# Splitting the MLP, the query and the turned rows between the GELUs of a two-layer transformer kernel

## The reference

```python
h = shift_token(x)                       # channels 128..255 from the row before
q, k, v = split(h @ wqkv)                # 8 heads of 64
q, k = l2norm(q) * qs, l2norm(k) * ksc
q, k = rotary_xpos(q, k)                 # x * cos + rotate_half(x) * sin, scaled
o = local_attention(q, k, v)             # windows of 128, each looks at itself and the one before
x = x + o @ wo
h = layernorm(shift_token(x)) * lg + lb
a, g = split(h @ w1 + b1)                # hidden width 682, padded to 6 blocks of 128
x = x + (a * gelu(g)) @ w2 + b2
```

## Time and profile before

| | us |
|---|---|
| median of 3 runs | 4432.98 (4428.99 to 4451.38) |
| the profiled execution | 4428.6 |
| its span, first to last instruction | 4426.8 |
| busy PE | 3827.8 (86%) |
| busy DVE | 2947.5 (67%) |
| busy ACT | 2631.8 (59%) |
| busy POOL | 1870.1 (42%) |

### The profile page before, as it was taken

One profiled execution on the slowest core, in us unless ns is written; L12 is line 12 of the kernel. 1 busy time (PEld: TensorE's weight loads), 2 busy tenths in 40 slices (PEclk: granted clock), 3 DMA queues, 4 the chain that ended last, 5 costly groups with the idle time before them and its releaser, 6 DMA issues. The chain is left out here.

```text
span 4426.8 us, 87646 instructions
## 1 busy us (share of the span) xinstructions
PE 3827.8 (86%) x33070; PEld 2945.5 (67%) x33070; DVE 2947.5 (67%) x7093; ACT 2631.8 (59%) x5752; POOL 1870.1 (42%) x1453
## 2 busy tenths in 40 slices
PE   4899999999987489989989998958999898989987
PEld 2454554554543378777878877847878787878776
DVE  5677777777773566766676666636676767676774
ACT  1455555555555366666666666636666666666674
POOL 2123233232230344445454545424555555555554
PEclk6899999999997699999999999978999999999999
DMA  5334434434420200000000000020000000000000
GB/s 133 81 65 117 96 72 116 102 76 108 118 45 24 79 14 16 18 14 19 14 19 14 19 16 16 10 70 8 23 22 24 21 24 21 25 21 23 22 23 20
DMA packets 145440, 195.90 MB, mean 44 GB/s; under 512 B 21532, under 2 KB 119544, under 8 KB 145024
## 3 DMA queue, kind: packets, MB, share of 16 engines
q1 hardware_dynamic: 145024, 190.31, 16.8%
HBM read 113.66 MB, written 67.16 MB: 41 GB/s over the span
## 5 line engine op out<-in xcount | busy, mean ns | idle before, releaser
L728 ACT ACTIVATE a_e_t<-a_ring 128x1024 f32<-128x1024 f32 (+3 forms) x768 | 611.3, 809 | 524.2 <-PE a_ring L869 365.9
L1622 POOL TENSOR_TENSOR b_e<-b_e,b_share 128x512 f32<-128x512 f32 (+1 forms) x512 | 502.5, 989 | 965.4 <-DVE b_share L2060 965.3
L1050 DVE TENSOR_REDUCE a_mx<-a_ring 128x2 f32<-128x1024 f32 (+3 forms) x768 | 724.6, 956 | 226.1 <-PE a_ring L869 112.3
L1730 ACT ACTIVATE b_e<-b_e,b_bias 128x256 f32<-128x256 f32 (+1 forms) x1024 | 494.4, 486 | 125.5 <-DVE b_bias L2052 122.8
L1607 POOL TENSOR_TENSOR b_qk_rot<-b_qk_rot,b_rot 128x512 f32<-128x512 f32 x256 | 373.2, 1479 | 308.6 <-DVE b_rot L2025 308.6
L2052 DVE CUSTOM_DVE_ANT_0 b_e<-b_bank_s,b_mask,b_inv 128x256 f32<-128x256 f32 (+1 forms) x1024 | 416.1, 462 | 39.1 <-PE b_bank_s L1885 39.1
L882 PE MATMUL a_ring<-a_k_st,a_q_st 48*128 48x512 f32 (+3 forms) x1536 | 327.8, 424 | 78.8 <-ACT a_e_t L728 41.5
L1740 ACT ACTIVATE b_e_t<-b_bank_et 128x512 f32<-128x512 f32 (+1 forms) x512 | 287.7, 562 | 146.2 <-PE b_bank_et L1896 144.7
L907 PE MATMUL a_ring<-a_q_st,a_k_st 50*128 50x512 f32 (+3 forms) x1536 | 340.9, 442 | 35.1 <-ACT a_e_t L728 13.9
L924 PE MATMUL a_outp<-a_e_t,a_v_t 128*32 128x512 f32 (+3 forms) x3072 | 340.1, 515 | 11.3 <-ACT a_e_t L728 6.2
L907 PEld LDWEIGHTS a_ring<-a_q_st,a_k_st 50*128 50x128 f32 x1536 | 148.0, 190 | 294.2 <-issue 151.3
(11 more groups left out here) (239 smaller groups left out, 11069.0 us busy)
## 6 DMA issues: line engine op xcount, KB each, us to landing
a_q_st<-a_parts_q SPq DMA_DIRECT2D x192, 128.0 KB, 4.7
a_k_st<-a_parts_k SPq DMA_DIRECT2D x192, 128.0 KB, 7.4
a_parts_q<-a_qk_p SPq DMA_DIRECT2D x16, 1024.0 KB, 8.3
a_parts_k<-a_qk_p SPq DMA_DIRECT2D x16, 1024.0 KB
b_fl<-f_rows SPq DMA_DIRECT2D x64, 256.0 KB, 4.1
a_xl<-in_L_attn_x SPq DMA_DIRECT2D x9, 1024.0 KB, 5.3
a_x<-in_L_attn_x SPq DMA_DIRECT2D x8, 1024.0 KB, 9.0
x_rows<-a_x SPq DMA_DIRECT2D x8, 1024.0 KB, 4.6
```

Source lines behind the costliest of these rows:

```text
L728: act.activation(e_t[:, step % 2, 2 * pair:2 * pair + 2, 0:cols], slot[:, :].rearrange("p (h t) -> p h t", h=2)[:, :, 0:cols], ACT.Exp).th ...
L1050: dve.reduce_max(mx[:, g % 2, :, pair, piece, t:t + 1], slot[:, :].rearrange("p (r c) -> p r c", r=2)[:, :, 0:cols], AX.X)\
L1622: pool.tensor_tensor(weights, weights, share[:, h % SPS, 2 * j:2 * j + 2].unsqueeze(2) .broadcast_to([P, 2, 2 * WIN - lo]), ALU.mult).then ...
L1730: ins = act.activation(weights, weights, ACT.Exp, scale=-1.0, bias=bias[:, h % SPS, at:at + 1], accum_out=total[:, h % SPS, at:at + 1])
```

## The change

- The GELUs' loop on ACT (`gelus`) now holds other work: after the third GELU the high part of the queries (`query_hi`, before this ahead of the loop) and the high part of the first half of the hidden values (`product_hi(u, 0)`, before this one phase later); after the fourth and fifth the high parts of the turned rows. DVE's `gated_products` holds the low parts of the queries and rows at the same places, and POOL's `product_lo(u, 0)` moves to the end of phase 0. The second half stays in phase 1.
- Turned rows go to the score banks s0 and s1, behind the turning of the queries. PE waits there for `row_tops` of the same step, and the next step's scores wait until the rows have been read.
- `rotation_products` does the queries' two products, then the keys' two, each with its own wait. The one product of 1024 columns becomes two of 512.
- POOL does both `share_out` of a step ahead of `unit_lo`; ACT does `unit_hi` behind the projections and the square rather than ahead of `values_hi`.
- DVE does `row_tops` ahead of `add_attention`. The moments of a unit's first window are taken at the end of phase 1 (`first_moments`), with a semaphore of their own.

```diff
@@ rows_hi, gelus (ACT)
-            def gelus(u):
+            def gelus(u, w, rows):
                 act.preload_act_table(ACT.Gelu)
                 for m in range(HK):
                     src, _ = filled(act, ("ag", u, m))
                     act.activation(ag[:, m, 1, :], src[:, UT:2 * UT], ACT.Gelu, bias=b1_c[:, 1, m:m + 1])\
                         .then_inc(gelu_done, 1)
+                    if m == HK // 2 - 1:
+                        if w is not None:
+                            query_hi(w)
+                        product_hi(u, 0)
+                    if HK // 2 <= m < HK // 2 + CK and rows:
+                        rows_hi(*rows, m - HK // 2)
...
-                u = frame.unit(g, NORM_AT)
-                if u is not None:
-                    unit_hi(u)
                 w = frame.window(g, OUT_AT)
                 if w is not None:
                     values_hi(w)
...
                     square(w)
+                u = frame.unit(g, NORM_AT)
+                if u is not None:
+                    unit_hi(u)
                 u = frame.unit(g - 1, AG_AT)
                 if u is not None:
-                    product_hi(u, 0)
                     product_hi(u, 1)
@@ turn_rows, scores (PE)
+                if frame.half(g) is not None:
+                    pe.wait_ge(tops_done, 2 * PPS * (g + 1))
...
+                if frame.rows(h - 1):
+                    for c in range(CK):
+                        taken(pe, ("fT", *frame.rows(h - 1), c))
@@ rotation_products (DVE)
-                taken(dve, ("q", w))
-                taken(dve, ("k", w))
-                cos = tab[:, :, 0, t, :].unsqueeze(2).broadcast_to([P, 2, H2, D2])
-                dve.tensor_tensor(qk_rot[:, :, :, :], qk[:, :, :, :], cos, ALU.mult)
-                for a in range(2):
+                for a, (what, turn) in enumerate((("q", "qT"), ("k", "kT"))):
+                    taken(dve, (what, w))
+                    cos = tab[:, a, 0, t, :].unsqueeze(1).broadcast_to([P, H2, D2])
+                    dve.tensor_tensor(qk_rot[:, a, :, :], qk[:, a, :, :], cos, ALU.mult)
@@ DVE's loop
+                h = frame.half(g)
+                if h is not None:
+                    row_tops(h)
                 out = frame.window(g - 1, OUT_AT)
                 if out is not None:
                     add_attention(out)
-                h = frame.half(g)
-                if h is not None:
-                    row_tops(h)
...
+                u = frame.unit(g + 1, MOMENTS_AT)
+                if u is not None:
+                    first_moments(u)
```

More of the change, by code:

```diff
@@ L1285, in plan_fills @@
 def plan_fills(frame):
-    banks = {name: [] for name in ("p", "t", "m0", "m1")}
+    banks = {name: [] for name in ("p", "t", "m0", "m1", "s0", "s1")}
     n_m = 0
@@ L1305, in plan_fills @@
         if frame.rows(g):
-            banks["t"].append(("fT", *frame.rows(g), 0))
-            banks["p"].append(("fT", *frame.rows(g), 1))
+            for c in range(CK):
+                banks[f"s{c}"].append(("fT", *frame.rows(g), c))
         w = frame.window(g, ROTATE_AT)
@@ L1444, in layer_stage @@
         shifted = [plain(f"shifted{n}") for n in range(2)]
+        shifted_first = [plain(f"shifted_first{n}") for n in range(2)]
         crossed = [plain(f"crossed{n}") for n in range(2)]
@@ L1653, in _ @@
                 if frame.half(g) is not None:
-                    share_out(g, 0)
+                    for j in range(PPS):
+                        share_out(g, j)
                 u = frame.unit(g, NORM_AT)
@@ L1657, in _ @@
                     unit_lo(u)
-                if frame.half(g) is not None:
-                    share_out(g, 1)
                 w = frame.window(g, PROJECT_AT)
@@ L1683, in _, with rows_hi @@
             steps = Steps(act, act_steps)
-            def rows_hi(i, half):
-                for c in range(CK):
-                    src, _ = filled(act, ("fT", i, half, c))
-                    act.activation(turned[0][:, c, 1 + 512 * half:513 + 512 * half], src[:, :], ACT.Copy)\
-                        .then_inc(f_hi, 1)
+            def rows_hi(i, half, c):
+                src, _ = filled(act, ("fT", i, half, c))
+                act.activation(turned[0][:, c, 1 + 512 * half:513 + 512 * half], src[:, :], ACT.Copy)\
+                    .then_inc(f_hi, 1)
             def take_projected(what, w):
@@ L1813, in _ @@
                     inverse_norms(w)
-                    query_hi(w)
+                u = frame.unit(g, AG_AT)
+                if u is not None:
+                    gelus(u, w, frame.rows(g))
+                else:
+                    if w is not None:
+                        query_hi(w)
+                    if frame.rows(g):
+                        for c in range(CK):
+                            rows_hi(*frame.rows(g), c)
                 u = frame.unit(g, MOMENTS_AT)
@@ L1817, in _ @@
                     inverse_deviations(u)
-                u = frame.unit(g, AG_AT)
-                if u is not None:
-                    gelus(u)
                 if w is not None:
@@ L1985, in _ @@
                     turn_qk("qT", w)
+                if frame.rows(g):
+                    turn_rows(g, *frame.rows(g))
                 u = frame.unit(g, AG_AT)
@@ L1992, in _ @@
                     second_products(u)
+                w = frame.window(g, ROTATE_AT)
                 if w is not None:
@@ L2127, in gated_products @@
                                              in1=ag[:, m, 1, :], op0=ALU.add, op1=ALU.mult).then_inc(back, 1)
+                    if m == HK // 2 - 1 and w is not None:
+                        query_lo(w)
+                    if HK // 2 <= m < HK // 2 + CK and rows:
+                        rows_lo(*rows, m - HK // 2)
             def add_unit(u):
@@ L2160, in _ @@
                     shares(h, 1)
-                if frame.rows(g):
-                    split_rows(*frame.rows(g))
                 if w is not None:
                     nearer_norms(w)
-                    query_lo(w)
+                u = frame.unit(g, AG_AT)
+                if u is not None:
+                    gated_products(u, w, frame.rows(g))
+                else:
+                    if w is not None:
+                        query_lo(w)
+                    if frame.rows(g):
+                        for c in range(CK):
+                            rows_lo(*frame.rows(g), c)
                 u = frame.unit(g, MOMENTS_AT)
```

54 lines of the change are left out of this document (26 added, 28 removed).

## The result

The changed kernel takes 4223.27 us (median of 4 runs, 4216.45 to 4225.78) against 4438.23 us of the kernel before beside it (4428.99 to 4451.38): a ratio of 0.9511, with a 95% interval of 0.9482 to 0.9540. The execution that was profiled took 4225.78 us, with a span of 4223.9 us. So the change won 202.9 us of span where 159 us were forecast, and the median lies 47 us under the forecast of 4270 us.

A forecast was written before the change was run, and what follows sets the result against it. The prediction took the layers to be bound by PE's work plus PE's gaps. Removed waits of 236 us, less 90 us given back, plus 13 us of clock make 159 us off 4428.6 us: 4270 us, range 4175 to 4350 us.

The forecast's parts named there:

- The four gains: Waits of PE that the change removes, as four terms: 108 + 50 + 64 + 14 = 236 us.
- The hidden values' low part: PE's wait in phase 2 for POOL's split goes, its first half now made in phase 0: 108 of 116.2 us.
- the output's low part: PE's wait in phase 3 goes, as values_hi no longer stands behind unit_hi on ACT: 50 of 55.0 us.
- the turned rows: PE's two waits at banks t and p go, with the rows in s0 and s1: 64 of 66.4 us.
- the gated products: PE's wait for banks they have not yet read shrinks, as the table load starts 0.58 us earlier: 14 of 24.9 us.
- The chain of the moments: Rotation, add_attention, shift, moments, normalisation come late: PE waits 0.6 us at the unit's turn, 0.8 at the weights; 90 us back.
- The first rival: DVE finishes both keys' products before POOL's addition, so the moments keep pace with PE: 4180 us, chance 0.25.
- The second rival: GELUs start late, since unit_hi behind the square delays unit_lo and POOL's additions: one us a unit, 4334 us, chance 0.20.
- Slower: The shift takes 9 us instead of 5.4 us, making 5 us of new waits a unit: 4513 us, chance 0.04.
- little change: PE's waits only change their name, as second half and shift come as late as PE: about 4420 us, chance 0.06.
- The clock: Falls of PE to 1.2 GHz cost at most 39 us over both layers; a third, 13 us, was counted as gained.

The follow-up runs named there:

- e7: The kernel before, with only the hidden values' first half split early, between the GELUs: 4358.25 us, ratio 0.9846 to before.
- e3: The changed kernel, with both halves of the hidden values split in phase 1 again: 4247.88 us, ratio 0.9575 to before.
- e6: The changed kernel, with unit_hi ahead of values_hi on ACT and unit_lo between the two share_out on POOL, as before: 4319.33 us.
- e1: The changed kernel, with add_attention put back ahead of row_tops on DVE: 4159.61 us, ratio 0.9373 to before.
- e2: The changed kernel, with the shift of 127 rows issued as two DMAs of 112 and 15 rows: 4160.65 us, ratio 0.9377 to before.
- e9: e8 without the lower bound on the sums of squares, a DVE operation on 16 columns in each window: 4135.64 us.
- e4: The changed kernel, with the rotation's cosine product joined again, one of 1024 columns for queries and keys behind both copies: 4213.35 us.
- e8: The changed kernel, with both add_attention ahead of row_tops and the shift as two DMAs of 112 and 15 rows: 4153.74 us.
- e5: The changed kernel, with the turned rows in banks t and p, ahead of the queries' turning, and their copies and subtractions at their old places: 4303.76 us.
- e10: e8 with the moments of a unit's first window taken directly ahead of the second's again, in phase 2: 4191.08 us.

## Why the prediction was right, and where its sizes were off

**The four gains** came out as computed. The hidden values' low part fell by 106.7 us (108 forecast), the output's low part by 48.8 us (50), the turned rows by 64.4 us (64), the gated products by 12.2 us (14): 232.1 us of waits against 236. As prices of single steps these sums are not the same thing: by e7 and e3 the early half is worth 64 us alone and 26 us at the end, by e6 the unit's place 106 us. Only because all four and the chain behind them were summed together did the total hold.

**The chain of the moments** was right in cause and in two of its three places. Forecast were 0.6 us at the unit's turn and 0.8 us at the weights, 90 us; measured, over the waits of before, are 20.6 us (28.6 - 8.0) and 38.9 us (44.9 - 6.0), plus 19.0 us (36.3 - 17.3) at the turned keys. That is 78.5 us, of which 59.5 us stand at the two places. The third place was missing: I had found the queries' turn with 0.5 us to spare and had not walked on to the keys', although the blocked operation stood in the earlier trace rows. PE that has waited there comes later to the unit's turn: 0.30 and 0.27 us in the unit above are together the 0.6 us that I had put at the turn alone. e1 and e2 show the first cause by its removal, e9 and e4 the second.

That the chain's length came out is in part luck, since two errors cancel. The first of the four products was blocked too, by POOL's `b_e` (1.32 us, where I had 0.64 us), so that the rotation took 4.2 us instead of 3.8. And the landing was read too long: the packets that still move from 2264.5 us on the earlier trace rows are not the shift's but those of the load of `fl`, which SP issues at 2261.28. The shift's packets, 512 bytes each to the load's 1024, end at 2264.34, 4.7 us after the issue and not 5.4. From issue to moments it took 5.1 us in the unit above, where I had 5.5.

**The first rival** (the chain keeps pace, 4180 us) fell on its condition: POOL does get in between two of DVE's products (1.76 us for the second one of the keys). Its time was reached, and passed, by different edits: e1 and e8 are at 4160 and 4154 us. Who goes first when both have work was left open in the prediction; here POOL's addition, which began at 2088.04 while DVE was at its third product, ran ahead of the fourth. The operation on 16 columns reads one operand from SBUF, where the prediction spoke of two, and is blocked all the same. The sum over `b_sq`, just ahead of it, is not: in e8 it takes 1198 to 1202 ns in all 58 windows of the first layer, although POOL's `b_hid_lo` of 1.85 us runs beside it in the ordinary unit.

**The second rival** (late GELUs) did not occur: the wait for `b_ag` fell from 24.9 to 12.7 us, and e6 shows that the old place of `unit_hi` made it longer, not shorter. "Slower" and "little change" did not occur; the shift still took 5.1 us from issue to moments.

**The clock is the mis-sized term.** I took a third of the 39 us that the granted clock could cost. In the bodies of the layers of the changed kernel it reads 1.00, here in the first and likewise from 2970 to 4190 us:

```profile
1600.00:2780.00 1180.00, 1135.21 (x9662) 1005.34 (x9661) 928.67 (x2597) 854.80 (x2164) 645.29 (x527) 1.00 0.06 17
```

against 0.99 and 0.98 of before. One fall of before, on PE and then by stretches of 1 us:

```profile
2043.89 0.40 PE L1836 MATMUL b_bank_m<-b_w_hi,b_hid_hi 128*128 128x256 f32 x1 [2.12 <-POOL b_hid_lo L1640]
2044.10 0.41 PE L1836 MATMUL b_bank_m<-b_w_lo,b_hid_hi 128*128 128x256 f32 x1
...
2047.50 0.28 PE L1836 MATMUL b_bank_m<-b_w_hi,b_hid_lo 128*128 128x256 f32 x1
2047.62 0.28 PE L1836 MATMUL b_bank_m<-b_w_hi,b_hid_hi 128*128 128x256 f32 x1
```
```profile
2044.00:2045.00 1.00, 1.00 (x6) 1.00 (x7) 0.45 (x1) 0.94 (x4) 1.00 (x1) 0.53 0.16 38
...
2048.00:2049.00 1.00, 1.00 (x11) 1.00 (x10) 0.53 (x4) 0.37 (x2) 0.54 (x1) 1.00 0.00 0
```

After a gap of 2.12 us the granted clock is 0.5, so 1.2 GHz, for some 3.5 us, and passes that follow one another every 0.12 us come every 0.21 us. So one long wait costs about 1.5 us a second time, as busy time (17 passes from 2043.89 to 2047.30, 0.09 us each). The bodies of before have 23 such falls (in 26 of their stretches of 20 us), those of the changed kernel two, both behind 4145 us. So 21 falls went, about 32 us by this price, of the bound of 39 us; I took 13.

What PE did before: 9 of the 23 falls come with the wait for the hidden values' low part (2.1 us, or 1.2 and 0.4 us), and 14 with the two waits around the turned rows, 1.03 and 1.20 us with 0.65 us of work between them. In e5, which brings this pair back (0.86 and 1.20 us), 8 of the 9 falls come with it. So these waits, too, cost more than the list says. Not every one is followed by a fall (7 of the 14 gaps of 2.1 us are, and 14 of the 28 pairs); why is not settled.

**A second part** of the busy time was not in the sum at all. In e6 the clock over the first body reads 1.00, and PE is still busier. Its row:

```profile
1600.00:2820.00 1220.00, 1139.96 (x9621) 997.45 (x9619) 936.34 (x2595) 854.05 (x2148) 638.51 (x522) 1.00 0.05 17
```

That is 118.5 ns a matmul (1139.96 / 9621), against 117.5 ns in the changed kernel (1135.21 / 9662); over the 20,755 of the layers 21 of the 25.4 us. It fits what a restart looks like in the earlier trace rows: the pass after a gap takes 0.35 us where 0.28 us are usual. I counted the two traces pass by pass, each against the median of the same pass in sequence. By this estimate the passes behind a gap carry about 30 us more in e6 than in the changed kernel, and those at the lower clock 3 us; no run separates the two. By the table each us of idle time went with 0.3 to 0.4 us of busy time in e1, e5 and e6 (15.2 / 42.5, 20.1 / 60.5, 25.4 / 80.3), but with far less in e10 (1.5 / 17.9) and more in e4 (9.0 / 10.8), so this is no price.

Taken together, the forecast was 44 us short of the span's gain (203 against 159). PE's busy time makes 34 of them (47.2 against 13), of which the clock is about 20, and the rest fits the passes behind gaps; the chain, forecast at 90 us and measured at 78.5, makes another 11.5.

## What to carry to other kernels

Sum the removed waits, but then walk one unit to the end with PE coming earlier, and price each arrival that no longer fits; that step took 90 us off a sum of 236 here, and it told where the next 60 us lay. Price the lower clock behind long waits as well: it was the term that was most too small. When such a chain is found in the working, look at once for the line of the change that lengthens it: putting `add_attention` back ahead of `row_tops` brings the time to 4160 us. A price from the list of waits is no price for an edit: the same cure was worth 64 us alone and 26 us beside the others, and by my reading of e3, e5 and e6 it depended on whether the wait stood inside the next chain or outside.

## What the runs showed of the hardware

- A DMA of 127 rows of 512 bytes between partitions ends 4.7 us after its issue and moves at about the share of one DMA engine of sixteen (0.08, 22 GB/s); as 112 and 15 rows it ends after 2.2 us.
- Some operations of DVE wait for a whole instruction of POOL: one on 16 columns, 0.17 us alone, took 1.03 us, a product of 0.68 us took 1.76 us. Leaving out the small one made the layers 23 us shorter (e8 to e9). A sum of 1.20 us that ran beside an instruction of POOL was not delayed.
- A pause of 2.1 us on PE was followed by 3.5 us at the lower clock, and removing the pauses brought the clock in the bodies to 1.00: about 32 us that no wait shows.
